# A list schedule with measured lengths and a random search over its ranks, in a fused macaron layer (feed-forward with eight experts, linear attention, feed-forward again)

## The reference

```python
x = x + 0.5 * _L0_ffn_ref(_layernorm(x, axis=-1), ...)
x = x + _L0_attn_ref(_layernorm(x, axis=-1), ...)
x = x + 0.5 * _L0_ffn_ref(_layernorm(x, axis=-1), ...)
```

```python
probs = jax.nn.sigmoid(logits)
scores, indices = jax.lax.top_k(probs, TOP_K)
scores = scores / jnp.sum(scores, axis=-1, keepdims=True)
```

## Time and profile before

| | us |
|---|---|
| median of 3 runs | 570.14 |
| lowest, highest | 568.78, 574.89 |
| the profiled execution | 569.31 |
| its span in the trace | 567.5 |
| PE busy, DVE busy | 486.3, 353.9 |
| POOL busy, ACT busy | 334.7, 280.6 |

### The profile page before, as it was taken

One profiled execution on the slowest core, in us unless ns is written; L12 is line 12 of the kernel. 1 busy time (PEld: TensorE's weight loads), 2 busy tenths in 40 slices (PEclk: granted clock), 3 DMA queues, 4 the chain that ended last, 5 costly groups with the idle time before them and its releaser, 6 DMA issues.

```text
span 567.5 us, 11032 instructions
## 1 busy us (share of the span) xinstructions
PE 486.3 (86%) x3056; PEld 402.5 (71%) x3056; DVE 353.9 (62%) x1059; ACT 280.6 (49%) x630; POOL 334.7 (59%) x338
## 2 busy tenths in 40 slices
PE   0958489999899999999999996989899998999920
PEld 0847478777777878888778775877787776778720
DVE  4688775633557675778887878788756353344331
ACT  4714346554655657556664465554364554355300
POOL 4355864076788676527788768735775764460072
PEclk9979799999999999999999999999999999999985
DMA  8931143243341333023213321123334434341121
GB/s 230 369 105 33 44 134 103 79 119 87 81 145 34 94 84 103 11 68 96 71 52 112 99 76 42 43 84 87 101 103 142 116 105 114 108 111 44 43 59 52
DMA packets 76041, 53.69 MB, mean 95 GB/s; under 512 B 9776, under 2 KB 70832, under 8 KB 75984
## 3 DMA queue, kind: packets, MB, share of 16 engines
q1 hardware_dynamic: 67792, 36.19, 22.0%
q0 software_dynamic: 8192, 16.79, 10.7%
HBM read 27.39 MB, written 25.56 MB: 93 GB/s over the span
## 4 chain that ended last, share of the span: by engine, by line
PE 74%; DVE 8%; issue 7%; ACT 4%; POOL 3%; DMA 2%; POOLq 0%; SPq 0%; DVEq 0%; ACTq 0%
PE gu L835 14%; PE gu L793 8%; PE ht_ps L826 7%; PE gu L795 7%; PE gu L794 7%; PE ht_ps L846 4%; PE gu L753 4%; PE gu L754 4%; PE gu L755 4%; PE xt_ps L776 3%; POOL yg L1145 2%; PE misc L855 2%; ACT gs L973 1%; PE misc L915 1%; PE misc L868 1%
## 5 line engine op out<-in xcount | busy, mean ns | idle before, releaser
L1145 POOL DMA_INDIRECT yg<-y_sorted,places x128 | 123.8, 967 | 107.0 <-PE gu L795 40.5
L1124 POOL DMA_INDIRECT x_sorted<-xn,places x128 | 128.5, 1004 | 84.5 <-PE gu L795 34.5
L835 PEld LDWEIGHTS gu<-w,hT 128*128 128x128 f32 x736 | 92.3, 191 | 24.0 <-issue 19.4
L835 PE MATMUL gu<-w,hT 128*128 x736 | 102.0, 281 | 6.2 <-ACT hT L979 4.0
L973 ACT ACTIVATE gs<-gu 128x512 f32<-128x512 f32 (+1 forms) x128 | 74.3, 582 | 63.7 <-PE gu L755 39.1
L793 PE MATMUL gu<-w,xbt_hi 128*128 x184 | 85.7, 466 | 6.8 <-ACT ys L954 3.9
L1192 DVE TENSOR_TENSOR hs<-gs,gu 128x512 f32<-128x512 f32 x96 | 63.2, 662 | 34.7 <-ACT gs L973 29.4
L1178 DVE TENSOR_TENSOR xbt_lo<-xt_ps,xbt_hi 128x256 fp32r<-128x256 f32 x96 | 39.4, 410 | 62.3 <-ACT xbt_hi L962 61.5
L795 PE MATMUL gu<-w,xbt_hi 128*128 x184 | 73.2, 398 | 0.0
L794 PE MATMUL gu<-w,xbt_lo 128*128 x184 | 73.2, 398 | 0.0
L979 ACT ACTIVATE hT<-ht_ps 128x512 f32<-128x512 f32 x96 | 55.6, 580 | 35.1 <-PE ht_ps L826 33.3
(11 more groups left out here) (132 smaller groups left out, 862.9 us busy)
## 6 DMA issues: line engine op xcount, KB each, us to landing
xb<-x_sorted SPq DMA_DIRECT2D x88, 128.0 KB, 2.2
y_sorted<-ys SPq DMA_DIRECT2D x88, 128.0 KB
X<-x_dram SPq DMA_DIRECT2D x8, 256.0 KB, 5.9
x_sorted<-yg SPq DMA_DIRECT2D x4, 512.0 KB, 6.7
x_sorted<-xn,places POOLq DMA_INDIRECT x128, 2.3
yg<-y_sorted,places POOLq DMA_INDIRECT x128, 2.6
out_dram<-X SPq DMA_DIRECT2D x8, 256.0 KB, 2.3
raw<-gate_w_dram SPq DMA_DIRECT2D x4, 256.0 KB, 4.6
```

Of the source, the lines that this page charges most:

```text
L835: mm = pe.matmul(dst[:, j * D:(j + 1) * D], hT[r % 2][:, at:at + P], w_flat[:, bass.ds(expert[r][j] + 2 * GU + half * D, D)], start=half = ...
L1124: nc.gpsimd.indirect_dma_start(x_sorted[l, g], bass.IndirectOffsetOnAxis(places[l, g][:, k, t:t + 1], 0), xn[:, b, t % T], None).then_inc( ...
L1145: nc.gpsimd.indirect_dma_start(yg[slot][:, k, t], None, y_sorted[l, g], bass.IndirectOffsetOnAxis(places[l, g][:, k, at:at + 1], 0)).then_ ...
```

## The change

Three things change, and the computation none.

The lengths in `describe`, `norm`, `unit`, `route`, `routed` and `attention` are replaced: on DVE, ACT and mostly on POOL by shorter ones, on PE by some shorter and some longer ones, and HOP, the time from one engine to another, goes from 14 to 16. Two lines stand for some sixty.

`search` runs the list scheduler 600 times. Each time the urgency of 1, 3, 10 or 40 families of pieces (one kind of piece for one sequence, group or unit) is shifted at random from the best so far, and the ranks with the shortest plan are kept. A trial in which no piece can begin is dropped.

`Once` stands between each engine's code and its semaphores: a wait for a value that this engine has already waited for on the same semaphore is not written. In the built program the instructions that do nothing but wait fall from 600 to 171 on PE, from 501 to 253 on ACT, from 418 to 92 on POOL and from 340 to 271 on DVE. No wait that orders anything goes.

```diff
-PACE, HOP, NEAR = 140, 14, 10
+PACE, HOP, NEAR = 140, 16, 10
+ROUNDS, SEED = 600, 1
...
-        op(("stats", l, b), "DVE", 125, *needs, ("moments", l, b - 1) if b else None)
+        op(("stats", l, b), "DVE", 80, *needs, ("moments", l, b - 1) if b else None)
...
-            op(("tap", b, j), "DVE", 80, ("tap", b, j - 1) if j > 1 else ("conv0", b))
+            op(("tap", b, j), "DVE", 64, ("tap", b, j - 1) if j > 1 else ("conv0", b))
...
+    def search(self):
+        serial = {key: n for n, key in enumerate(self.ops)}
+        plain = {key: (self.urgency(key), self.stage(key), serial[key]) for key, o in self.ops.items() if o[0]}
+        family = {key: self.family(key) for key in plain}
+        families = sorted(set(family.values()), key=str)
+        rng = np.random.default_rng(SEED)
+        best, shift = None, {}
+        for n in range(ROUNDS):
+            trial = dict(shift)
+            if n:
+                for i in rng.integers(len(families), size=rng.choice((1, 3, 10, 40))):
+                    trial[families[i]] = rng.normal(0, 1.2) if rng.random() < 0.8 else 0
+            rank = {key: (u + trial.get(family[key], 0), *more) for key, (u, *more) in plain.items()}
+            if self.schedule(rank) and (best is None or max(self.end.values()) <= best[0]):
+                best, shift = (max(self.end.values()), rank), trial
+        self.schedule(best[1])
...
+        class Once:
+            def __init__(self, eng):
+                self.eng, self.reached = eng, {}
+
+            def wait_ge(self, s, value):
+                if value > self.reached.get(s, 0):
+                    self.reached[s] = value
+                    self.eng.wait_ge(s, value)
...
             def pair_turn(r):
-                pe.wait_ge(xb_loaded[r % XB], 16 * (r // XB + 1))
-                wait(pe, xbt_lo_done, r)
+                once.wait_ge(xb_loaded[r % XB], 16 * (r // XB + 1))
+                wait(once, xbt_lo_done, r)
```

More of the change, by code:

```diff
@@ L138, in norm @@
             free += tuple(("scatter", 1, g, n) for n in range(2 * tiles(1, g)))
-        op(("norm", l, b, 0), "ACT", 98, ("shift", l, b), *free)
-        op(("norm", l, b, 1), "ACT", 98, ("norm", l, b, 0))
+        op(("norm", l, b, 0), "ACT", 80, ("shift", l, b), *free)
+        op(("norm", l, b, 1), "ACT", 80, ("norm", l, b, 0))
         op(("turn", l, b), "PE", 45, ("norm", l, b, 1), ("const",))
-        op(("hi", l, b), "ACT", 60, ("turn", l, b))
-        op(("lo", l, b), "DVE", 69, ("hi", l, b))
+        op(("hi", l, b), "ACT", 50, ("turn", l, b))
+        op(("lo", l, b), "DVE", 60, ("hi", l, b))
         if l != 2:
             op(("logits", l, b), "PE", 90, ("lo", l, b), ("cut_router_lo",))
-            op(("bias", l, b), "DVE", 50, ("logits", l, b))
+            op(("bias", l, b), "DVE", 33, ("logits", l, b))
     def shared(self, l, b):
@@ L205, in experts @@
                 done = [("gather", l, b, n)]
-            op(("add", l, b, "first"), "DVE", 155, ("gather", l, b, 2 * T - 1), ("weigh", l, g))
-            op(("add", l, b, "second"), "DVE", 155, ("add", l, b, "first"))
+            op(("add", l, b, "first"), "DVE", 106, ("gather", l, b, 2 * T - 1), ("weigh", l, g))
+            op(("add", l, b, "second"), "DVE", 106, ("add", l, b, "first"))
     def routed(self, r, l, g, n):
@@ L241, in attention @@
         self.unit(vg, ("front", q, 0))
-        op(("k_tok", b), "ACT", 60, ("front", kv, 0), last("rope_sin"), *(("cut_w_lo", e) for e in range(E)))
-        op(("v_tok", b), "ACT", 60, ("front", kv, 0), last("kv"))
-        op(("rope_cos", b), "POOL", 130, ("k_tok", b), last("kv"))
+        op(("k_tok", b), "ACT", 49, ("front", kv, 0), last("rope_sin"), *(("cut_w_lo", e) for e in range(E)))
+        op(("v_tok", b), "ACT", 49, ("front", kv, 0), ("k_tok", b), last("kv"))
+        op(("rope_cos", b), "POOL", 124, ("k_tok", b), last("kv"))
@@ L264, in attention @@
+        op(("rdenT", b), "ACT", 18, ("rden_turn", b), last("spread"))
+        op(("spread", b), "PE", 108, ("rdenT", b))
+        op(("rden_bc", b), "ACT", 50, ("spread", b), last("attend"))
         op(("num", b), "PE", 90, ("spread", b))
-        op(("attend", b), "DVE", 75, ("num", b), ("rden_bc", b), ("vT", b), last("gate"))
-        op(("gate", b), "DVE", 145, ("attend", b), ("tap", b, TAPS - 1), ("og", b), last("project"))
+        op(("attend", b), "DVE", 66, ("num", b), ("rden_bc", b), ("vT", b), last("gate"))
@@ L267, in attention @@
+        op(("gate", b), "DVE", 132, ("attend", b), ("tap", b, TAPS - 1), ("og", b), last("project"))
         op(("project", b), "PE", 90, ("gate", b))
-        op(("attended", b), "DVE", 69, ("project", b))
+        op(("attended", b), "DVE", 60, ("project", b))
     HELD = {"turn": "lo", "logits": "bias", "count": "based", "kv": "mask", "den": "invert", "rden_turn": "rdenT",
@@ L324, in freed, with family, schedule @@
         return {"Q": (("q_cos", b), ("q_sin", b)), "VG": (("vT", b), ("og", b)), "KV": (("v_tok", b), ("v_tok", b))}[u[2]]
-    def schedule(self):
+    def family(self, key):
+        return (key[0], *key[1][0:3]) if key[0] in ("front", "silu", "hid") else key[0:3]
+    def search(self):
[14 more added lines that the diff above has]
+        self.schedule(best[1])
+    def schedule(self, rank):
         ops, end, start = self.ops, {}, {}
         self.start, self.end = start, end
+        self.order = {e: [] for e in ("PE", "ACT", "DVE", "POOL", "SP")}
         self.units, self.hidden, self.shared_order, self.turn_order = [], [], [], []
-        self.order = {e: [] for e in ("PE", "ACT", "DVE", "POOL", "SP")}
         self.misc, self.xt_of, self.yg_of = {}, {}, {}
@@ L466, in schedule @@
                     best = (t, serial[key], key, engine, t)
-            assert best, ("no piece can begin", sorted(waiting, key=str)[:20])
+            if not best:
+                return False
             _, _, key, engine, t = best
@@ L676, in _ @@
         def _(sp):
+            once = Once(sp)
             def load_x(b):
@@ L1107, in pace @@
                 half_through, through = plan.through(key)
-                wait(pool, half_ready, half_through)
-                wait(pool, gu_ready, through)
+                wait(once, half_ready, half_through)
+                wait(once, gu_ready, through)
             def scatter(l, g, n):
```

363 lines of the change are left out of this document (182 added, 181 removed).

## The result

The changed kernel takes **569.6 us** (median of 20 runs, 564.8 to 575.1) against 570.9 (20 runs, 568.1 to 575.4) of the kernel before in the same group: ratio 0.994, 95% interval 0.9915 to 0.9966. The ratio is worked out from the fast executions alone, so it is not the quotient of the two medians. Two later groups gave 0.9963 (0.9919 to 1.0007) and 1.0006 (0.997 to 1.0042). So the change is worth between nothing and 0.9%. The forecast was 544.3, and its range ended at 535 and 557; within 1% of no change it had given a chance of 0.05.

The account below looks back on a forecast made before the run. PE was taken to bound the kernel, busy 86% of the span, so time is its work plus its losses. From 569.3 us, 12 (start), 9 (end), 4 (middle), 0 (elsewhere) and 0 (waits) came off: 544.3, range 535 to 557.

Parts of the forecast that it names:

- The start: Before the first routed matmul: an earlier routing and scatter chain cuts PE's losses, gain 12 us, bounds 5 and 15.5.
- The lower bound of 5: Start, before the first routed matmul: the chain moves but PE keeps some 25 us of losses, gain 5 us.
- The end: After the last routed product: 10.0 us of PE work moves beside POOL's gathers, gain 9 us, bounds 6 and 10.
- The middle: Attention of the last two sequences, 340 to 372 us: 4 of 6.5 us PE idle gained, bounds 0 and 6.5.
- Elsewhere: PE's idle outside start, end and middle: no change, 0 us, bounds -4 (gain) and +8 (loss).
- The failure sign: Between first and last routed pair: prediction is wrong if PE's idle grows from 26.5 to over 35 us.
- The waits: Repeated waits left out, mostly on POOL and PE: gain 0; 4.8 us if half of each POOL gap were waits.
- The slower one: Attention: DVE and POOL exclusion holds up taps in each of eight sequences, 4.0 us each, time 576 us; chance 0.03.
- Only the end: Order buys only the end: start gives 5, end 8, middle nothing, time 556 us; chance 0.17.

Follow-up runs that it names:

- f1: The changed kernel itself run again (new lengths, search with seed 1), ordinary chip: 570.0 us, ratio 0.9963 to the kernel before.
- i1: The changed kernel itself run once more in a later group, ordinary chip: 570.5 us, ratio 1.0006 to the kernel before.
- i2: The changed kernel with ACT's four lengths of a pair put back, DVE's two left short, ordinary chip: 555.4 us, ratio 0.9761.
- g1: The changed kernel with six lengths of a routed pair's ACT and DVE steps put back, seed 1: 543.9 us, ratio 0.9525.
- g2: Old lengths with the search, seed 1, but the pair's six lengths as short as in the changed kernel: 572.1 us, ratio 1.0055.
- f4: The changed kernel with seed 2 of the random search instead of seed 1: 560.6 us, ratio 0.983 to the kernel before.
- g3: Old lengths with the search, seed 2, repeated waits left out, against the kernel before: 553.3 us, ratio 0.9724.
- h1: The changed kernel without the search (plain list), the pair's six lengths put back, long chip: 618.5 us, ratio 0.9427.
- f2: The kernel before with only the repeated waits left out (old order and lengths, no search), ordinary chip: 567.2 us, ratio 0.9923.
- groups e and h: The two groups of runs, called the long chip, in which every kernel took longer; the kernel before took 653 to 654 us.
- e1: The kernel before with only the repeated waits left out (old order and lengths, no search), long chip: 638.5 us, ratio 0.9804.

## Why the prediction was wrong

**The start: 12 forecast, 5.3 in the first profile, 1 in two others.** The chain moved as worked out: first scatter 43.59 (43 to 44 forecast), no roots among 16 scatters, last cut done at 71.2 (70.4). The first routed matmul came at 79.7 instead of 72.3, since that chain was no longer what came last. PE lost 25.0 us ahead of it, not 18.3, against 30.3 before. In two later profiles of the same kernel (f1, i1) it came at 84.2 and 84.3, and 29.3 to 29.4 were lost; in f1 the granted clock is at the lower of its two levels from 77.2 to 87.4 us. I had added 6.9 us of work to PE's queue there and costed it at full clock and without waits. It stood behind a `turn`'s wait for DVE and an `sdown` at low clock. The lower bound of 5 named this case, and the later profiles lie below it.
The wait of DVE for POOL did stay. Four small operations between 29.2 and 39.7 us took 1.34, 0.97, 1.25 and 1.25, and two more were caught near 70, which the forecast had looked for only at the routing: the cuts moved behind the scatters meet the next group's routing and a layernorm's shift. The row of `shifts<-mv,rstd` has 1.05 us beside a cut on POOL, where the median of the 24 instructions of its line is 0.15; a reduction with one input at 30.58, beside the first cuts, takes 0.22 like the other 15 of its line. The Trainium skill, "SBUF — State Buffer", "Who interferes with whom", says that a VectorE instruction with two SBUF inputs contends with a GpSimd one that reads SBUF; the trace agrees in both.

**The end: 9 forecast.** The move came as said: 23.2 us busy of 25.8 after 530, gathers 1.26 apart and not held by `pace`. From the last routed product to the end of the span it is 31.8 us (32.8 before; I had said 33 to 35), with PE busy for 19.1 of them. That the 10 us left the dense phase is right, and that they made it shorter is wrong, see below.

**The middle: 4 forecast.** From 340 to 372 PE's idle fell by 5.4 us, with no wait over 2 us before Wo.

**Elsewhere: 0 forecast, and this is the step that failed.** It read "I take 0, bounds -4 (gain) and +8 (loss), since nothing shows a price for it: DVE's shorter lengths leave less room between the engines' queues". The right place, and the wrong size: it names DVE, where ACT's four lengths are over half of the loss (i2). The sum took the dense phase as work plus a constant loss, so that every microsecond of work moved out would come off the time. The phase had 17 us less work and took as long: 8.8 us more in gaps, 1.5 in late second matmuls, 4.6 in slow starts (6.5 more of these at the low clock), and 1.4 in the rest. Since the middle gained its 5.4 us inside this phase, the term elsewhere was a loss of some 20 us, where I had 0 with a bound of 8. Six lengths are the cause (g1, g2, f4 and g3 with another seed, h1). Put back, the same search gives 543.9, next to the forecast's 544.3. That is partly luck: from the first routed matmul to the last routed product g1 takes 433.0 us where the forecast's terms make 435.5, but its first routed matmul comes at 79.3 and not at 72.3, and the left-out waits gave 4.4 that I had not counted. What I could have read: the lengths were in the diff, and the durations of those very steps in the profile, 0.1 us longer each.
The failure sign that I gave, PE's idle between first and last pair growing from 26.5 to over 35, was not reached: it is 31 to 32. The loss is partly inside what the profile calls busy, which an idle sum does not see.

**The waits: 0 forecast, 4.4 measured** (f2). The upper bound was 4.8. The reason given for zero, POOL's constant gap, did hold: 0.30 us with one wait or four. So the gain is elsewhere; in f2 the first scatter is 1.4 us earlier and the phase of routed pairs 1.4 shorter, spread over the program and in no one place. Why is open. On the long chip it is 2%.

**The rivals.** The slower one (576) came nearest in time, with the mechanism of DVE and POOL in attention; attention is where the change did best, so that is luck. "Only the end" (556) was 14 us off. None had the dense phase as its place, with its idle time already known to be small; that is why a range of 535 to 557 missed.

**What the change is made of:** waits -4.4, new lengths +20 (587.0 against 567.2), the search on them -17 (570.0 against 587.0). The steps come from two groups and are each taken from the one before, so their sum of -1.4 only says again that the changed kernel is level with the kernel before. In another order they have other sizes: on the old lengths the search is worth -21. Best of all is the change with a pair's six lengths put back: **543.9 us**, 4.7% faster than the kernel before.

What stays open: whether the old lengths help as time of the engine or as time until the result (HOP 30, which gives only the second, was 626.4 on the long chip, ahead of the plain lists, and was not run beside g1), whether the length of the copy `hT` does it alone, what DVE's two are worth, what makes the gaps that stay in i2, and what the idle times of groups e and h are.

## What to carry to other kernels

Lengths in a plan that are above an engine's start-to-start time can hold room for the hand-over. Here the lists without it cost PE 21 us in the dense phase, of which only 7.5 show as idle time (the change against g1). Change a plan's costs apart from the search that uses them, and count the hand-overs that start straight on their producer. Time two seeds before a list is called better: here two lists of one kind differ by 7 to 9 us, 1.3 to 1.7%.

## What the runs showed of the hardware

A `down` that waits for its input starts 0.14 us after the copy's end, and its second matmul 0.208 after the first instead of 0.112: about 0.1 us on top of the wait, counted as busy, and 5.2 us in the whole dense phase of the change. The Trainium skill, "TensorE: Matmul & The Clock Gate", "Step-by-step: what each phase is for", has the next weights loaded while the matmul before runs; the trace agrees where the weights are there in time (0.112 apart, with loads of 0.19 us each under them), and shows what is lost where they aren't.

ACT takes up its next instruction 0.49 us after the start of one whose result takes 0.60 (94.17 and 94.66), so one instruction has two lengths, how long it keeps the engine and how long its result takes.

Leaving out the repeated waits of one and the same order was worth 0.8% in one group (f2, 0.9897 to 0.9949) and 2% in another (e1, 0.9744 to 0.9863), though the median gap between POOL's DMAs stayed 0.30 us in both.
